# Beginning of a graph-plus-LSTM kernel: the item bias row spread over the partitions by its transfer, nine products of ones ahead of the item quads, and VectorE's first low part ahead of its first item sum

## The chip, the core and the metric

The kernel runs on one core of a Trainium2 chip. The metric is the device time of one execution in microseconds, the median of the runs shown; lower is better.

## The reference

What is computed, cut to what matters here:

```python
# x: 10000 x 128, adj: 10000 x 10000, item_feat: 10000 x 128, all float32
h = item_feat @ W_item.T + b_item              # "items": 10000 x 128, b_item: 128
b = layernorm(x) @ W_user.T + b_user
x = x + relu(adj @ h + b)
x = x + ffn(layernorm(x)[None])[0]             # a one-layer LSTM of 10000 steps, gating, running sums
```

The change concerns the first line only: the bias `b_item`, one row of 128 numbers, is added to every row of the item product.

## The kernel before

**Stages.** The first 1100 us or so compute `adj @ h` for 20 blocks of 500 users (`BW = 500`), with the layer norms and the user product of each block beside it. The items are held as 78 chunks of 128 rows and a tail of 16. For each block, 20 "pieces" of up to 4 chunks of the transposed adjacency stream from memory into `raw` (4 slots). Each piece is worked in two halves of 2 chunks (128 x 1000 numbers): ScalarE rounds a half to its high part `a_hi` (`split_hi`), VectorE subtracts to get the low part `a_lo` (`split_lo`), and TensorE makes three products for each chunk, high x high, low x high and high x low, into `psG` (lines 884 to 886). ScalarE and VectorE write into 4 rotating buffers (`CUT = 4`), so the high part of a later half waits for the products of the half four before it. After the adjacency comes the recurrence.

**The items in block 0.** The items are made during the first block, four chunks (a "quad") at a time: `item_quad(q)` on TensorE writes `psI` (two buffers) from the item features, which land in `u` in ten parts; `item_sum_part(q)` on VectorE adds the bias `bi` and writes `u`; `item_hi_part(q)` on ScalarE rounds to `item_hi`; `item_lo_part(q)` on VectorE subtracts to `item_lo`. The first three adjacency products of a piece need the quad that holds its chunks, high and low (`item_ready`). An item quad is 4 products of 128 x 128 in plain float32, which the profile shows as 8 weight loads and 8 matmuls.

**The beginning.** The order on every engine is written out by hand, and the engines meet by semaphores alone.
- SyncE's queue issues item part 0, then both halves of adjacency piece 0, item part 1, and on.
- ScalarE's queue issues the item weights `wi`, the bias row, the first block of x (`xb`), the user weights `wu` and the user bias. Then ScalarE loads its table and works on half pieces and item high parts as they become ready.
- TensorE makes 8 products of a tile of ones (`keep_at_work(WARM_UP)`, results unused), the bias product, quads 0 and 1, 5 products of ones (`WARM_ON`), the 6 products of the first half piece, quad 2, and on.
- The bias comes as one row into partition 0 (`bi_row`). A product of a row of ones with it (line 944, one row deep) puts the bias into all 128 partitions of the PSUM buffer `psW`, and VectorE copies it to `bi` (line 1336). The row shares its place with `x1_rows`, by which name the trace calls it (`x_rows`).

A product of float32 by float32 appears as two loads and two matmuls, so 8 products of ones are "x16" in the trace.

Of the kernel before, what the change touches and what calls it, by code (L numbers as in the profile page):

```python
# [26 lines left out]
P = 128  # L27
N = 10000
HID = 128
# [43 lines left out]
HI_ONLY = [(q, part) for part in (0, 2) for q in range(4)]  # L73
LO_ONLY = [(q, 1) for q in range(4)]
KEEP_WARM = 8
WARM_UP, WARM_ON = 8, 5
BETWEEN = 4
HANDOVER_TOL = 2.0 ** -19
assert K * L == N and OW % L == 0 and L % 8 == 0 and OW >= 3 * L
# [12 lines left out]
def program(nc, xT, itemT, adj_main, adj_tail, w_itemT, b_item, w_userT, b_user, w_ihT, w_hhT,  # L92
# [13 lines left out]
    with ctx:  # L106
        def sb(name, shape, dt=f32, where=ctx):
            return where.enter_context(nc.sbuf_tensor(name, shape, dt))

        def pb(name, shape, where=ctx):  # L110
            return where.enter_context(nc.psum_tensor(name, shape, f32))

        def sem(name):
            return ctx.enter_context(nc.semaphore(name))
# [5 lines left out]
        ones = sb("ones", [P, P])  # L120
# [5 lines left out]
        bi = sb("bi", [P, HID])  # L126
# [29 lines left out]
        x1_rows = sb("x1_rows", [P, SUB * HID], f32, first)  # L156
        x1b = x1_rows[:, 0:BW]
        wu = x1_rows[:, 0:HID]
        bi_row = x1_rows[0:1, HID:2 * HID]
        normed = x1_rows  # L160
        v_hi = sb("v_hi", [P, BW], f32r, first)
        v_lo = sb("v_lo", [P, BW], f32r, first)
# [16 lines left out]
        psW = pb("psW", [P, 512], first)  # L179
# [44 lines left out]
        wi_in = sem("wi_in")  # L224
        item_tail_ready = sem("item_tail_ready")
        bi_in = sem("bi_in")
        bi_psum = sem("bi_psum")
        bi_ready = sem("bi_ready")
        wu_in = sem("wu_in")
        w_in = sem("w_in")  # L230
        wx_in = sem("wx_in")
# [112 lines left out]
        def cols(c0, n=1):  # L344
            return slice(c0 * BW, (c0 + n) * BW)
# [239 lines left out]
        def _(act):  # L585

            act.dma_start(wi[:, :], w_itemT).then_inc(wi_in, 16)
            act.dma_start(bi_row[:, :], b_item[0:1, :]).then_inc(bi_in, 16)
            act.dma_start(xb[:, 0, :], xT[:, cols(0)]).then_inc(x_in[0], 16)
            act.dma_start(wu[:, :], w_userT).then_inc(wu_in, 16)  # L590
            act.dma_start(bu[:, :], b_user).then_inc(wu_in, 16)
# [262 lines left out]
        def _(pe):  # L854
# [64 lines left out]
            def item_quad(q):  # L919

                if q == 0:
                    pe.wait_ge(wi_in, 16)
                if q in PARTS:
                    pe.wait_ge(item_in[PARTS.index(q)], 16)
                if q >= 2:
                    pe.wait_ge(item_sum, q - 1)
                if q == QUADS - 1:
                    pe.wait_ge(item_tail_ready, 1 + len(STACK))
                for c in range(4 * q, min(4 * q + 4, CH + 1)):
                    rows = P if c < CH else STACKED  # L930
                    columns = u[:, L + c * P:L + (c + 1) * P] if c < CH else item_tail[:, :]
                    last = pe.matmul(psI[0:rows, q % 2, (c % 4) * HID:(c % 4 + 1) * HID], columns, wi[:, :],  # L932
                                     start=True, stop=True)
                last.then_inc(item_psum, 1)
# [5 lines left out]
            pe.wait_ge(ones_ready, 1)  # L940
            keep_at_work(WARM_UP)
            pe.wait_ge(const_ready, 6)
            pe.wait_ge(bi_in, 16)
            pe.matmul(psW[:, 0:HID], ones[0:1, :], bi_row[:, :], start=True, stop=True).then_inc(bi_psum, 1)
            item_quad(0)
            item_quad(1)
            keep_at_work(WARM_ON)
# [176 lines left out]
            with pe.If(redo > 0):  # L1124
                pe.wait_ge(g_restored, 2)
                with nc.tensor.Fori(0, K) as k:
                    with nc.tensor.Fori(0, L) as l:
                        pe.wait_ge(g_h, k * L + l + 1)
                        for q in range(4):
                            for k2, t in enumerate((u_hi, u_lo)):  # L1130
# [3 lines left out]
                                             start=False, stop=True)  # L1134
# [9 lines left out]
        def _(dve):  # L1144
# [32 lines left out]
            def low_user(j):  # L1177
                dve.wait_ge(v_hi_ready, j + 1)
                dve.tensor_tensor(v_lo[:, :], v, v_hi[:, :].bitcast(f32), ALU.subtract).then_inc(v_lo_ready, 1)
# [38 lines left out]
            def item_sum_part(q):  # L1218

                n = min(4, CH + 1 - 4 * q)  # L1220
                dve.wait_ge(item_psum, q + 1)
                if q < QUADS - 1:
                    dst = u[:, L + 4 * q * P:L + (4 * q + n) * P]
                    dve.tensor_tensor(dst.rearrange("p (c h) -> p c h", h=HID),  # L1224
                                      psI[:, q % 2, 0:n * HID].rearrange("p (c h) -> p c h", h=HID),
                                      bi[:, :].unsqueeze(1).to_broadcast([P, n, HID]), ALU.add)\
                        .then_inc(item_sum, 1)
                    return

                dve.memset(sq[:, 0:n * HID], 0.0).then_inc(prep, 1)  # L1230
                dve.wait_ge(prep, 1)
                for c0, c1, a, b in ((0, n - 1, 0, P), *((n - 1, n, a, a + TAIL) for a in STACK)):
                    dve.tensor_tensor(sq[a:b, c0 * HID:c1 * HID].rearrange("p (c h) -> p c h", h=HID),
                                      psI[a:b, q % 2, c0 * HID:c1 * HID].rearrange("p (c h) -> p c h", h=HID),
                                      bi[a:b, :].unsqueeze(1).to_broadcast([b - a, c1 - c0, HID]), ALU.add)\
                        .then_inc(item_sum if a == STACK[-1] else prep, 1)
                dve.wait_ge(prep, 4)

            def item_lo_part(q):
                n = min(4, CH + 1 - 4 * q)  # L1240
                src = u[:, L + 4 * q * P:L + (4 * q + n) * P] if q < QUADS - 1 else sq[:, 0:n * HID]
                dve.wait_ge(item_hi_ready, q + 1)
                last = dve.tensor_tensor(item_lo[:, 4 * q * HID:(4 * q + n) * HID], src,  # L1243
                                         item_hi[:, 4 * q * HID:(4 * q + n) * HID].bitcast(f32), ALU.subtract)
                if q == QUADS - 1:
                    low = slice(STACK[-1], STACKED)
                    own_hi = item_hi[low, CH * HID:(CH + 1) * HID]
                    last.then_inc(prep, 1)
                    dve.wait_ge(prep, 5)
                    last = dve.tensor_tensor(own_hi, sq[low, (n - 1) * HID:n * HID], own_hi.bitcast(f32), ALU.subtract)  # L1250
                last.then_inc(item_ready, 1)
# [31 lines left out]
            def body(j, has2=True, has1=True, items=False):  # L1283
                for r in range(PIECES):
                    if not has1:
                        prepare(r)
                    split_lo(j, r, 0)
                    if items and r == 0:
                        item_lo_part(0)
                        item_sum_part(1)  # L1290
                    if items and 0 < r < QUADS - 2:
                        item_sum_part(r + 2)
                    split_lo(j, r, 1)
                    if items and r == 0:
                        item_sum_part(2)
                    if items and r + 1 < QUADS:
                        item_lo_part(r + 1)
                    if items and r == FIRST["stats"]:
                        stats(0)
                        pair_up(0)  # L1300
                        eps(0)
                    if items and r == FIRST["centred"]:
                        dve.wait_ge(wu_psum, 1)
                        dve.tensor_scalar(wu_hi[:, :], psW[:, 0:HID], 1.0, None, ALU.mult).then_inc(wu_ready, 1)
                        dve.wait_ge(wu_ready, 1)
                        dve.tensor_tensor(wu_lo[:, :], psW[:, 0:HID], wu_hi[:, :].bitcast(f32), ALU.subtract)\
                            .then_inc(wu_ready, 1)
                    if items and r == FIRST["scaled"]:
                        scale_user(0)
                    if r == (FIRST if items else AT)["v_lo"]:  # L1310
                        low_user(j)
                    if has2 and r == AT["scaled"]:
                        scale_user(j)
                    if has2 and r == AT["x1"]:
                        add_relu(j - 1)
                    if has2 and r == AT["stats2"]:
                        stats(2 * j)
                    if has2 and r == AT["pair2"]:
                        pair_up(2 * j)
                    if has2 and r == AT["eps2"]:  # L1320
                        eps(2 * j)
                    if has2 and r == AT["scale2"]:
                        row_scale(2 * j)
                    if has2 and r == AT["apply2"]:
                        apply_rstd(j)
                    if has2 and r == AT["shift2"]:
                        apply_shift(j)
                    if has1 and r == AT["stats1"]:
                        stats(2 * j + 1)
                    if has1 and r == AT["pair1"]:  # L1330
                        pair_up(2 * j + 1)
                    if has1 and r == AT["eps1"]:
                        eps(2 * j + 1)

            dve.wait_ge(bi_psum, 1)
            dve.tensor_copy(bi[:, :], psW[:, 0:HID]).then_inc(bi_ready, 1)
            dve.wait_ge(bi_ready, 1)
            item_sum_part(0)
            body(0, has2=False, items=True)

            body(1)
# [301 lines left out]
```

## Time and profile before

| | |
|---|---|
| median of 3 runs | 1427.13 us (1426.66 to 1427.23) |
| the profiled execution | 1430.41 us |
| its span, first to last instruction | 1428.6 us |
| TensorE busy (PE) | 1405.4 us, 98% of the span |
| weight loads busy (PEld) | 1215.2 us, 85% |
| VectorE busy (DVE) | 1272.8 us, 89% |
| ScalarE busy (ACT) | 1055.8 us, 74% |
| mean granted TensorE clock | 0.993 of full speed |
| read from memory | 432 MB, 310 GB/s over the span |

PE is TensorE's matmuls, PEld its weight loads, which overlap the matmuls; DVE is VectorE, ACT ScalarE, SP SyncE. A "q" behind an engine's name (SPq, ACTq) marks its instruction queue, which issues the transfers. The ends of matmuls are modelled, so the starts of the weight loads are the better clock of what TensorE does. A busy share is a mean over stages: what matters for a change in the first 13 us is which wait ends last there.

### The profile page before, as it was taken

The numbers are of one execution on the slowest core, as the hardware profiler recorded it, in microseconds if no ns is written. First come the engines' busy times: TensorE is split into PE (matmuls) and PEld (weight loads), VectorE is DVE, ScalarE is ACT, GpSimd is POOL, SyncE is SP. The second block draws the span as 40 slices with busy tenths as digits, with TensorE's granted clock in tenths as the row PEclk, the third lists the DMA queues.
The fourth block names the chain that finished last, engine by engine and source line by source line (L and its number), as shares of the span: only waits on it lengthen the run. The fifth ranks groups of instructions, "written<-read, shape, count | busy, mean of one in ns | idle before, by whom it ended". The sixth has DMA issues, their size and how long they took to land.

```text
span 1428.6 us, 26247 instructions
## 1 busy us (share of the span) xinstructions
PE 1405.4 (98%) x7464; PEld 1215.2 (85%) x7464; DVE 1272.8 (89%) x2102; ACT 1055.8 (74%) x1449; POOL 210.0 (15%) x189
## 2 busy tenths in 40 slices
PE   9999999999999999999999999999999999999995
PEld 8878888888888888888888888888888899999994
DVE  7999999999999999999999999999999766676666
ACT  6677787787777777877887877877877676556663
POOL 0000100000000000001001001001000131037775
PEclk9999999999999999999999999999999999999997
DMA  9999999999999999999999999999999203000003
GB/s 375 354 346 379 403 389 387 399 391 374 404 391 382 403 387 381 401 388 398 384 392 392 397 381 402 390 381 401 391 379 386 102 0 144 0 1 1 0 0 144
DMA packets 143466, 442.96 MB, mean 310 GB/s; under 512 B 23944, under 2 KB 43337, under 8 KB 143307
## 3 DMA queue, kind: packets, MB, share of 16 engines
q1 hardware_dynamic: 126048, 426.43, 77.1%
q10 hardware_dynamic: 17387, 16.14, 3.9%
q8 instruction: 17, 0.28, 0.1%
q14 instruction: 14, 0.11, 0.0%
HBM read 432.15 MB, written 10.36 MB: 310 GB/s over the span
## 4 chain that ended last, share of the span: by engine, by line
PE 94%; DVE 5%; ACT 0%; issue 0%; POOL 0%; DVEq 0%; ACTq 0%; POOLq 0%
PE psG L884 24%; PE psG L885 24%; PE psG L886 24%; PE psZ L989 10%; PE psZ L977 3%; PE psZ L975 3%; PE psZ L979 3%; DVE a_lo L1210 2%; PE psZ L995 1%; PE psT L859 1%; PE psI L932 1%; DVE u L1525 1%; DVE item_lo L1243 0%; DVE u L1224 0%; PE psV L938 0%; PE psG L877 0%
## 5 line engine op out<-in xcount | busy, mean ns | idle before, releaser
L667 ACT ACTIVATE a_hi<-raw 128x1000 fp32r<-128x1000 f32 (+1 forms) x800 | 819.1, 1030 | 240.4 <-PE psG L886 222.5
L1210 DVE TENSOR_TENSOR a_lo<-raw,a_hi 128x1000 fp32r<-128x1000 f32 (+1 forms) x800 | 897.0, 1170 | 19.3 <-ACT a_hi L667 14.7
L884 PE MATMUL psG<-a_hi,item_hi 128*128 128x500 f32 x1560 | 610.3, 391 | 1.4 <-DVE a_lo L1210 1.4
L885 PE MATMUL psG<-a_lo,item_hi 128*128 128x500 f32 x1560 | 605.5, 388 | 0.0
L886 PE MATMUL psG<-a_hi,item_lo 128*128 128x500 f32 x1560 | 604.1, 387 | 0.0
L884 PEld LDWEIGHTS psG<-a_hi,item_hi 128*128 128x128 f32 x1560 | 293.2, 188 | 63.3 <-DVE a_lo L1210 2.4
L886 PEld LDWEIGHTS psG<-a_hi,item_lo 128*128 128x128 f32 x1560 | 292.8, 188 | 59.4
L885 PEld LDWEIGHTS psG<-a_lo,item_hi 128*128 128x128 f32 x1560 | 293.3, 188 | 55.5
L989 PE MATMUL psZ<-hist,wh 128*128 (+1 forms) x1264 | 167.9, 276 | 2.9 <-DVE hist L1363 2.2
L989 PEld LDWEIGHTS psZ<-hist,wh 128*128 128x128 f32 x1264 | 154.7, 192 | 3.8 <-issue 2.4
L468 POOL TENSOR_TENSOR row_terms<-var,minus_half 125x4 f32<-125x4 f32 x20 | 37.6, 1879 | 679.8 <-DVE var L1161 679.8
L721 ACT ACTIVATE psZ<-psZ 128x250 f32<-128x250 f32 x158 | 57.3, 363 | 63.6 <-PE psZ L989 61.6
L977 PE MATMUL psZ<-u_lo,wx_hi 128*128 (+1 forms) x312 | 97.9, 315 | 0.0
L975 PE MATMUL psZ<-u_hi,wx_hi 128*128 (+1 forms) x312 | 93.8, 302 | 0.0
L979 PE MATMUL psZ<-u_hi,wx_lo 128*128 (+1 forms) x312 | 87.5, 282 | 0.0
L468 POOL TENSOR_TENSOR rstd<-var,minus_half 125x4 f32<-125x4 f32 x20 | 34.9, 1743 | 331.4 <-DVE var L1161 331.4
L1348 DVE SCALAR_TENSOR_TENSOR psZ<-psZ,C 128x125 f32<-128x125 f32 x158 | 46.6, 295 | 35.8 <-ACT psZ L721 34.7
L1363 DVE SCALAR_TENSOR_TENSOR hist<-go,psZ 128x125 f32 (+1 forms) x160 | 45.5, 284 | 35.0 <-ACT psZ L730 34.4
L725 ACT ACTIVATE go<-psZ 128x250 f32<-128x250 f32 x158 | 59.4, 376 | 6.6 <-PE psZ L989 0.3
L730 ACT ACTIVATE psZ<-C 128x125 f32<-128x125 f32 x158 | 43.6, 276 | 24.2 <-DVE C L1358 20.7
L977 PEld LDWEIGHTS psZ<-u_lo,wx_hi 128*128 128x128 f32 x312 | 59.4, 191 | 0.8
L979 PEld LDWEIGHTS psZ<-u_hi,wx_lo 128*128 128x128 f32 x312 | 59.1, 190 | 0.8
(188 smaller groups left out, 865.4 us busy)
## 6 DMA issues: line engine op xcount, KB each, us to landing
raw<-in_adj_main SPq DMA_DIRECT2D x760, 500.0 KB, 6.7
raw<-in_adj_main SPq DMA_DIRECT2D x40, 250.0 KB, 5.5
sq<-rstd_copy ACTq DMA_DIRECT2D x20, 250.0 KB, 6.7
u<-x_copy SPq DMA_DIRECT2D x1, 5000.0 KB, 14.5
x_copy<-x_rows SPq DMA_DIRECT2D x19, 250.0 KB, 7.2
sq<-rows_copy ACTq DMA_DIRECT2D x19, 250.0 KB, 6.1
un_bb<-rows_copy ACTq DMA_DIRECT2D x19, 250.0 KB, 7.6
u<-in_itemT SPq DMA_DIRECT2D x9, 512.0 KB, 9.4
```

The source lines that it names most:

```text
L468: pool.tensor_tensor(t[:, :], var[:, :], minus_half[0:SW, :].to_broadcast([SW, SUB]), ALU.pow).then_inc(ln_rstd, 1)
L667: nc.scalar.activation(a_hi[:, s % CUT, 0:n], raw[:, r % RAW, at:at + n], ACT.Copy)\
L721: nc.scalar.activation(tb(g, 0, 2).rearrange("p (q k) -> p q k", k=KG), zb(g, 0, par), ACT.Tanh)\
L725: nc.scalar.activation(go[:, g, :].rearrange("p (q k) -> p q k", k=KG), zb(g, 1, par), ACT.Tanh)\
L884: pe.matmul(bank, w_hi, hi, start=(c == 0), stop=False)
L885: pe.matmul(bank, w_hi, lo, start=False, stop=False)
L886: last = pe.matmul(bank, w_lo, hi, start=False, stop=False)
L975: pe.matmul(z, w_hi, hi, start=(q % 2 == 0), stop=False, skip_group_check=True)
L977: pe.matmul(z, w_hi, lo, start=False, stop=False, skip_group_check=True)
L979: pe.matmul(z, w_lo, hi, start=False, stop=False, skip_group_check=True)
L989: last = pe.matmul(psZ[:, 2 * par + bank, at:at + KG], wh[:, q * HID:(q + 1) * HID], hist[:, row, g * KG:(g + 1) * KG], start=False, stop= ...
L1210: last = dve.tensor_tensor(a_lo[:, s % CUT, 0:m], raw[:, r % RAW, at:at + m], a_hi[:, s % CUT, 0:m].bitcast(f32), ALU.subtract)
```

## The change

1. **The bias.** The transfer itself now spreads the row over the 128 partitions: each of 128 rows of `bi` is read from the same 512 bytes in memory. The product on TensorE, the copy on VectorE and two semaphores go. VectorE waits for the transfer (`bi_in`) ahead of its first item sum.
2. **The warm-up.** Nine products of ones ahead of the item quads, instead of eight and the bias product.
3. **VectorE's order.** The first low part of the adjacency, `split_lo(0, 0, 0)`, comes first, and the first item sum behind it.

```diff
--- before.py
+++ after.py
@@ -73,7 +73,7 @@
 HI_ONLY = [(q, part) for part in (0, 2) for q in range(4)]
 LO_ONLY = [(q, 1) for q in range(4)]
 KEEP_WARM = 8
-WARM_UP, WARM_ON = 8, 5
+WARM_UP, WARM_ON = 9, 5
 BETWEEN = 4
 HANDOVER_TOL = 2.0 ** -19
 assert K * L == N and OW % L == 0 and L % 8 == 0 and OW >= 3 * L
@@ -156,7 +156,6 @@
         x1_rows = sb("x1_rows", [P, SUB * HID], f32, first)
         x1b = x1_rows[:, 0:BW]
         wu = x1_rows[:, 0:HID]
-        bi_row = x1_rows[0:1, HID:2 * HID]
         normed = x1_rows
         v_hi = sb("v_hi", [P, BW], f32r, first)
         v_lo = sb("v_lo", [P, BW], f32r, first)
@@ -224,8 +223,6 @@
         wi_in = sem("wi_in")
         item_tail_ready = sem("item_tail_ready")
         bi_in = sem("bi_in")
-        bi_psum = sem("bi_psum")
-        bi_ready = sem("bi_ready")
         wu_in = sem("wu_in")
         w_in = sem("w_in")
         wx_in = sem("wx_in")
@@ -585,7 +582,7 @@
         def _(act):
 
             act.dma_start(wi[:, :], w_itemT).then_inc(wi_in, 16)
-            act.dma_start(bi_row[:, :], b_item[0:1, :]).then_inc(bi_in, 16)
+            act.dma_start(bi[:, :], b_item[0:1, :].to_broadcast([P, HID])).then_inc(bi_in, 16)
             act.dma_start(xb[:, 0, :], xT[:, cols(0)]).then_inc(x_in[0], 16)
             act.dma_start(wu[:, :], w_userT).then_inc(wu_in, 16)
             act.dma_start(bu[:, :], b_user).then_inc(wu_in, 16)
@@ -940,8 +937,6 @@
             pe.wait_ge(ones_ready, 1)
             keep_at_work(WARM_UP)
             pe.wait_ge(const_ready, 6)
-            pe.wait_ge(bi_in, 16)
-            pe.matmul(psW[:, 0:HID], ones[0:1, :], bi_row[:, :], start=True, stop=True).then_inc(bi_psum, 1)
             item_quad(0)
             item_quad(1)
             keep_at_work(WARM_ON)
@@ -1286,6 +1281,8 @@
                         prepare(r)
                     split_lo(j, r, 0)
                     if items and r == 0:
+                        dve.wait_ge(bi_in, 16)
+                        item_sum_part(0)
                         item_lo_part(0)
                         item_sum_part(1)
                     if items and 0 < r < QUADS - 2:
@@ -1332,10 +1329,6 @@
                     if has1 and r == AT["eps1"]:
                         eps(2 * j + 1)
 
-            dve.wait_ge(bi_psum, 1)
-            dve.tensor_copy(bi[:, :], psW[:, 0:HID]).then_inc(bi_ready, 1)
-            dve.wait_ge(bi_ready, 1)
-            item_sum_part(0)
             body(0, has2=False, items=True)
 
             body(1)
```

VectorE's first instructions, before; `a_lo` is the low part of a half piece, `u<-psI,bi` an item sum, `item_lo` an item low part, and brackets hold the semaphores that an instruction waits for:

```order
L1336 COPY bi<-psW 128x128 [waits bi_psum]
L1224 TENSOR_TENSOR u<-psI,bi 128x512 [waits item_psum,bi_ready]
L1210 TENSOR_TENSOR a_lo<-raw,a_hi 128x1000 [waits hi_ready]
L1243 TENSOR_TENSOR item_lo<-u,item_hi 128x512 [waits item_hi_ready]
L1224 TENSOR_TENSOR u<-psI,bi 128x512 [waits item_psum]
L1210 TENSOR_TENSOR a_lo<-raw,a_hi 128x1000 [waits hi_ready]
L1224 TENSOR_TENSOR u<-psI,bi 128x512 [waits item_psum]
L1243 TENSOR_TENSOR item_lo<-u,item_hi 128x512 [waits item_hi_ready]
```

And now (line numbers are 5 lower):

```order
L1205 TENSOR_TENSOR a_lo<-raw,a_hi 128x1000 [waits hi_ready]
L1219 TENSOR_TENSOR u<-psI,bi 128x512 [waits item_psum,bi_in]
L1238 TENSOR_TENSOR item_lo<-u,item_hi 128x512 [waits item_hi_ready]
L1219 TENSOR_TENSOR u<-psI,bi 128x512 [waits item_psum]
L1205 TENSOR_TENSOR a_lo<-raw,a_hi 128x1000 [waits hi_ready]
L1219 TENSOR_TENSOR u<-psI,bi 128x512 [waits item_psum]
L1238 TENSOR_TENSOR item_lo<-u,item_hi 128x512 [waits item_hi_ready]
```

The copy is gone, and the low part of half 0 moved ahead of the first sum; from the first `item_lo` on both orders are the same.

TensorE's first instructions, before (`psV<-ones` are the products of ones, `psW<-x_rows,ones` the bias product, `psI` the item quads, `psG` the adjacency products):

```order
L938 MATMUL psV<-ones 128x128 [waits ones_ready]
L938 MATMUL psV<-ones 128x128 x7
L944 MATMUL psW<-x_rows,ones 128x128 [waits bi_in,const_ready]
L932 MATMUL psI<-wi,u 128x128 [waits item_in0,wi_in]
L932 MATMUL psI<-wi,u 128x128 x7
L938 MATMUL psV<-ones 128x128 x5
L884 MATMUL psG<-a_hi,item_hi 128x500 [waits lo_ready,item_ready]
L885 MATMUL psG<-a_lo,item_hi 128x500
```

And now (line numbers are 3 lower):

```order
L935 MATMUL psV<-ones 128x128 [waits ones_ready]
L935 MATMUL psV<-ones 128x128 x8
L929 MATMUL psI<-wi,u 128x128 [waits item_in0,wi_in,const_ready]
L929 MATMUL psI<-wi,u 128x128 x7
L935 MATMUL psV<-ones 128x128 x5
L881 MATMUL psG<-a_hi,item_hi 128x500 [waits lo_ready,item_ready]
L882 MATMUL psG<-a_lo,item_hi 128x500
```

The bias product with its wait for the bias row is gone, one product of ones is added, and the wait for the constants moved to quad 0.

ScalarE's and SyncE's queues keep their order; in ScalarE's, the second transfer is now `bi<-in_b_item 128x128`.

## Rows read from the trace of the kernel before

**Rows 1.** Windows: busy us by engine (instructions), granted clock, DMA share, GB/s.

```profile
5.43:8.80 3.37, 3.37 (x17) 3.37 (x17) 1.47 (x3) 1.49 (x2) 0.00 (x0) 1.00 1.04 410
...
13.02:80.00 66.98, 66.50 (x361) 56.20 (x359) 66.41 (x99) 46.34 (x55) 3.51 (x6) 1.00 0.97 361
...
86.00:1123.00 1037.00, 1036.55 (x4667) 863.40 (x4666) 986.98 (x1278) 812.36 (x833) 69.98 (x39) 1.00 1.01 388
...
1284.00:1288.00 4.00, 3.29 (x20) 3.09 (x21) 2.44 (x8) 2.93 (x8) 1.88 (x3) 0.81 0.00 0
```

**Rows 2.** The chain that ended last, 5 to 20 us: start, us, what.

```profile
9.21 1.51 PE psV L938 x10
...
13.02 0.69 DVE u L1224
```

**Rows 3.** Timeline, 0 to 45 us: start, us, engine, what, idle before.

```profile
0.75 0.39 SPq L397 DMA_DIRECT2D u<-in_itemT  x1
0.75 0.41 ACTq L587 DMA_DIRECT2D wi<-in_w_itemT  x1
...
1.19 0.91 SPq L409 DMA_DIRECT2D raw<-in_adj_main  x2
...
1.20 0.54 ACTq L588 DMA_DIRECT2D x_rows<-in_b_item  x1
...
1.77 0.38 ACTq L589 DMA_DIRECT2D xb<-in_xT  x1
...
2.18 0.51 ACTq L590 DMA_DIRECT2D x_rows<-in_w_userT  x1
...
5.99 1.04 ACT L667 ACTIVATE a_hi<-raw 128x1000 fp32r<-128x1000 f32 x1 [1.02 <-DMA raw<-in_adj_main]
...
7.62 0.69 DVE L1224 TENSOR_TENSOR u<-psI,bi 128x512 f32<-128x512 f32 x1 [1.79 <-PE psI L932]
8.23 1.19 DVE L1210 TENSOR_TENSOR a_lo<-raw,a_hi 128x1000 fp32r<-128x1000 f32 x1
8.35 0.63 ACT L705 ACTIVATE item_hi<-u 128x512 fp32r<-128x512 f32 x1 [1.32 <-DVE u L1224]
...
9.34 0.68 DVE L1243 TENSOR_TENSOR item_lo<-u,item_hi 128x512 fp32r<-128x512 f32 x1
...
13.02 0.69 DVE L1224 TENSOR_TENSOR u<-psI,bi 128x512 f32<-128x512 f32 x1 [1.30 <-PE psI L932]
```

**Rows 4.** Timeline of TensorE's weight loads, 0 to 12 us.

```profile
1.00 3.48 PEld L938 LDWEIGHTS psV<-ones 128*128 128x128 f32 x16 [1.00 <-POOL ones L455]
4.71 0.50 PEld L944 LDWEIGHTS psW<-x_rows,ones 1*128 1x128 f32 x2 [0.22 <-issue]
5.43 3.49 PEld L932 LDWEIGHTS psI<-wi,u 128*128 128x128 f32 x16 [0.23 <-issue]
8.80 1.74 PEld L938 LDWEIGHTS psV<-ones 128*128 128x128 f32 x10
10.46 0.19 PEld L884 LDWEIGHTS psG<-a_hi,item_hi 128*128 128x128 f32 x1
...
11.71 0.41 PEld L932 LDWEIGHTS psI<-wi,u 128*128 128x128 f32 x2
```

**Rows 5.** Transfers by line: KB each, us from issue to landing.

```profile
u<-in_itemT SPq DMA_DIRECT2D x1, 512.0 KB, 4.0
wi<-in_w_itemT ACTq DMA_DIRECT2D x1, 64.0 KB, 4.1
...
raw<-in_adj_main SPq DMA_DIRECT2D x1, 500.0 KB, 4.8
...
xb<-in_xT ACTq DMA_DIRECT2D x1, 250.0 KB, 6.3
...
x_rows<-in_w_userT ACTq DMA_DIRECT2D x1, 64.0 KB, 7.4
```

**Rows 6.** Timeline of TensorE's weight loads, 10.3 to 10.5 us.

```profile
10.12 0.41 PEld L938 LDWEIGHTS psV<-ones 128*128 128x128 f32 x3
```

## Prediction

> **What bounds the kernel now.** I began with windows of the span. From 86 us to 1123 us TensorE is busy 1036.55 of 1037 us [rows 1]. The reader is to see that nothing in the beginning can change what that stretch costs; it can only make it start earlier or later. From 13.02 to 80 us VectorE is busy 66.41 of 66.98 us and TensorE 66.50 [rows 1]: both are close to full, so a shift of the whole pattern passes through to the end, and a shift of one engine alone would not.
>
> So the question is what sets the start of VectorE's unbroken work. The chain that ended last runs through TensorE's queue, the late warm-up products among it, into VectorE's third item sum at 13.02 [rows 2]. VectorE had waited 1.30 us for that sum [rows 3], and everything of it follows from there.
>
> Under that chain lie the weight loads of TensorE [rows 4] and the timeline of VectorE and ScalarE [rows 3]. The first big product's load began at 10.46. Its two conditions were met before: the low part of item quad 0 ended at 9.34 + 0.68 = 10.02, the low part of the first half piece at 8.23 + 1.19 = 9.42. So TensorE's own queue came last: quad 0 began only at 5.43, and the five products behind quad 1 ended at about 10.46. That is the queue from which the change takes the bias product.
>
> **The change, part by part.**
>
> *The bias product on TensorE.* Its two loads began at 4.71, and the first load of quad 0 at 5.43; ahead of each stands a short idle time, 0.22 and 0.23 us, that no recorded event explains [rows 4]. Now a ninth product of ones fills a part of that place. One load every 3.37 / 16 = 0.211 us (5.43 to 8.80 for 16) lets 18 loads end at 1.00 + 3.80 = 4.80. The first item transfer landed at 0.75 + 4.0 = 4.75, the item weights at 0.75 + 4.1 = 4.85 [rows 3, 5]. So quad 0 can begin at 4.89 at the earliest, and at 5.43, as before, if the stall comes with the waits and not with the bias product. I take 5.0, by the landings, which are the nearer rows. Both quads then end at 5.0 + 3.37 = 8.37.
>
> *The clock.* The granted clock stands at 1.00 for 5.43 to 8.80 too [rows 1], yet loads came every 0.21 us there and every (0.41 - 0.19) / 2 = 0.11 us from 10.12 on [rows 6]: the levels of 1.2 and of 2.4 GHz. Ten loads from 8.80 to 10.46 are about six at 0.21 and four at 0.11, which puts the rise near 9.9. Until then TensorE had worked without a pause since 5.43, and had paused twice before that. With the rise at 9.9 again, the ten loads now are seven at 0.21 and three at 0.11: they end at 8.37 + 1.80 = 10.17. With an earlier rise they end earlier still; with quad 0 at 5.43 they end at 10.46 as before.
>
> *VectorE's order.* The copy of the bias goes; it lay inside VectorE's wait for quad 0, 1.79 us that ended at 7.62 [rows 3], and is worth nothing. The low part of the first half piece now stands ahead of the first item sum. It can start when ScalarE's high part is done, 5.99 + 1.04 = 7.03, plus a hand-over of 0.04 (the first sum ended at 7.62 + 0.69 = 8.31, ScalarE's item high part began at 8.35): 7.07. The next instruction starts 1.11 later (8.23 to 9.34): the first sum at 8.18, which is 0.56 **later** than the 7.62 of before, although quad 0 is done sooner. From there: sum done 8.87; item high part on ScalarE 8.91 to 9.54; item low part on VectorE 9.58 to 10.26, against 10.02 before. Before, that low part was held back by the adjacency's until 9.34, 9.34 - 8.98 = 0.36 after its own input was ready; now it waits for its input. With 0.05 for the hand-over the first big product begins at 10.31.
>
> *The sum.* TensorE's queue is free at 10.17, VectorE's item low part allows 10.31: the last wait has changed hands, and the gain is 10.46 - 10.31 = 0.15 us, or 0 if quad 0 still begins at 5.43. The path behind keeps its length: six big products 11.71 - 10.46 = 1.25 [rows 4], then quad 2, and the third sum 13.02 - 10.46 = 2.56 after the first big product, at 12.87. VectorE is there in time: after the item low part at 9.58 come the second sum at 10.18 and the second low part at 10.78, and it is free at 11.89. So 0.98 us of its old 1.30 of idle time is left, and that cover also hides a second sum that would come 0.9 late.
>
> *The bias by its transfer.* It stays second in ScalarE's queue, but moves 64 KB in 128 rows and not 0.5 KB in one. The transfers around it bound its landing: as fast as the item weights (64 KB, 4.1 us) it lands at 1.20 + 4.1 = 5.30; as slow as the user weights (64 KB, 7.4 us) at 8.60, 0.42 after the sum wants it [rows 3, 5]. I take about 5.5 to 6: it stands right behind the item weights, and ahead of x, which landed at 1.77 + 6.3 = 8.07. So it is hidden by the low part, which keeps VectorE until 8.18. Issuing 128 rows took ScalarE 0.41, the one row 0.54: no loss there.
>
> What it may push is the first half piece of the adjacency, which landed at 1.19 + 4.8 = 5.99 [rows 3, 5] and from which the new path now hangs. Lower bound 0: x was waiting in ScalarE's queue in any case, so the bias takes x's place in time, not the half piece's. Between: 64 KB at 410 GB/s [rows 1] is 0.16 us. Upper bound: the user weights, also 64 KB, landed at 2.18 + 7.4 = 9.58, 1.5 us behind x; were the half piece held back as long, everything would move by 1.5. I take 0, for the first reason.
>
> The Trainium skill, "DMA: Bandwidth & Descriptors", section "Bandwidth", calls transfers under 64 KB dominated by their descriptors and measures 0.95 us for 64 KB; by it, were all of that ahead of the half piece, the result would be 0.95 - 0.15 = 0.8 us slower. The same page's section "Queues, rings and completion order" has a DMA engine alternate between the queues that have work, which is how I read it above; no row here tells the two apart.
>
> Against what time: the profiled execution took 1430.41 us, 1.8 of it outside its span of 1428.6, and stands 3.3 above the median of 1427.13. Some of that may be in its late part, where the granted clock was 0.81 between 1284 and 1288 us [rows 1]; the beginning has none in it. I take 0.15 off the median: 1427.0 us.
>
> **The rivals.**
>
> *A, the forecast: VectorE's chain takes over, a small gain.* Between 1427.13 (none) and 1426.9. Chance 0.66.
>
> *B: the clock is the prize.* The timed runs need not have had the rise at 9.9. Where it comes only after quad 2, the old path pays 4 loads of 0.10, 1.25 for six big products at half the rate and 8 loads of 0.10: 2.45 us. With the pauses filled the rise may come before that: 1427.13 - 0.15 - 2.45 = 1424.5 at best, about 1425.8 if half the runs had it. For it: the pauses ahead of quad 0 are the only ones before the rise. Against it: the three runs lie within 0.57 us, which a clock that moves the path by 2.45 would spread; and with the rise of the profiled run, an earlier one gives nothing beyond A, since the first sum waits for the low part until 8.18 however soon quad 0 is done. Chance 0.12. The Trainium skill, "TensorE: Matmul & The Clock Gate", section "What's actually happening", has the throttled state as the default and activity as what releases it; the trace agrees in so far as the loads grow shorter after an unbroken stretch.
>
> *C: slower, through the first half piece.* The bias transfer holds back its landing by more than 0.15 us, or itself lands after 8.33. Time: from 1427.15 up to 1427.0 + 1.5 = 1428.5. For it: before, the low part could have begun at 7.07 and began at 8.23, so the half piece had 1.16 to spare, and now it has nothing. Against it: x's place in the queue. Chance 0.16.
>
> *D: the time moves by more than the beginning can make it,* in either direction, by the late clock or by how the changed code lies. Chance 0.06.
>
> **How the numbers follow.** 0.2% of 1427 is 2.85 us, about what a measurement of this kernel can tell from no change. A, B and C lie inside it. Faster by over 0.2%: 0.01 of B, where the slow stretch is longer than I priced, and 0.03 of D: 0.04. Slower: 0.03 of D. Within: 0.93. The range of 1425.4 to 1428.3 takes A, most of C and two thirds of B. With the spread of the three runs, A's own range is 1426.6 to 1427.4.
>
> **What would show it.** In the new trace: no copy on VectorE; quad 0's first load near 5.0; the adjacency low part at 7.07, the first sum at 8.2, the item low part ending near 10.26; the first big product near 10.31, released by the item low part and not by TensorE's own queue; the third sum at about 12.87. Loads every 0.11 us before 9 us would be B's clock. ScalarE's first high part after 6.1, or a first sum that waits for a transfer, would be C and make me wrong, as would a third sum before 12.6.

## The result: 0.25% slower

| | before | changed |
|---|---|---|
| median of 12 runs | 1427.39 us (1426.44 to 1431.05) | 1431.2 us (1430.0 to 1433.1) |
| profiled execution, its span | 1430.41, 1428.6 | 1430.81, 1429.0 |

The ratio is 1.0025, with a 95% interval from 1.0017 to 1.0033: 3.6 us slower, between 2.4 and 4.7. I had forecast 1427.0 and a range up to 1428.3.

The two spans differ by 0.4 us only, so the spans alone would have hidden the loss. Read from the front, the traces agree with the medians. In the timeline of TensorE's weight loads of either kernel, at the first products of the recurrence, the changed kernel is 1131.72 - 1128.08 = 3.64 us behind:

```profile
1128.08 0.52 PEld L989 LDWEIGHTS psZ<-hist,wh 128*128 128x128 f32 x4 [0.84 <-DVE hist L1363]
```

```profile
1131.72 0.41 PEld L984 LDWEIGHTS psZ<-hist,wh 128*128 128x128 f32 x3 [0.84 <-DVE hist L1356]
```

Two things behind the changed part then favoured the changed kernel's profiled run. The clock that was down around 1286 us in the kernel before [rows 1] stayed up in it, and late in the recurrence the same weight load is only 1408.14 - 1406.07 = 2.07 us behind. And between VectorE's last instruction (at 1422.91 and 1424.97) and the end of the span lie 5.7 and 4.0 us. Each is worth about 1.6 us, and neither goes with the beginning: of the 13 traces here, five have the long end and eight the short one, and two (the kernel before and e12) have the low clock near 1286 us. The same may happen in the runs that were only timed, which spread over as much as 5.1 us for one kernel (e12); no trace shows those. This is why the experiments below are read first by places in the trace.

The profile after. VectorE's timeline (start, us, engine, what, idle before), which answers to [rows 3]:

```profile
9.01 1.20 DVE L1205 TENSOR_TENSOR a_lo<-raw,a_hi 128x1000 fp32r<-128x1000 f32 x1 [9.01 <-ACT a_hi L664]
10.13 0.68 DVE L1219 TENSOR_TENSOR u<-psI,bi 128x512 f32<-128x512 f32 x1
11.51 0.69 DVE L1238 TENSOR_TENSOR item_lo<-u,item_hi 128x512 fp32r<-128x512 f32 x1 [0.69 <-ACT item_hi L702]
...
16.27 0.69 DVE L1219 TENSOR_TENSOR u<-psI,bi 128x512 f32<-128x512 f32 x1 [2.36 <-PE psI L929]
```

The third sum stands at 16.27 and not at 13.02. ScalarE's first high part, in its timeline, waited 2.98 us for its half piece and began at 7.94, not 5.99:

```profile
7.94 1.04 ACT L664 ACTIVATE a_hi<-raw 128x1000 fp32r<-128x1000 f32 x1 [2.98 <-DMA raw<-in_adj_main]
```

TensorE's weight loads, against [rows 4]:

```profile
1.00 3.91 PEld L935 LDWEIGHTS psV<-ones 128*128 128x128 f32 x18 [1.00 <-POOL ones L452]
5.03 2.39 PEld L929 LDWEIGHTS psI<-wi,u 128*128 128x128 f32 x16
7.33 1.20 PEld L935 LDWEIGHTS psV<-ones 128*128 128x128 f32 x10
12.25 0.19 PEld L881 LDWEIGHTS psG<-a_hi,item_hi 128*128 128x128 f32 x1 [3.72 <-DVE item_lo L1238]
...
13.49 0.33 PEld L883 LDWEIGHTS psG<-a_hi,item_lo 128*128 128x128 f32 x1
```

Quad 0 did begin at 5.03, and the clock rose sooner: the 16 loads of the quads took 2.39 us in place of 3.49. But then TensorE was idle for 3.72 us, and a load at 13.49 takes 0.33 us again. Windows of the changed kernel (as [rows 1], the last three numbers being granted clock, DMA share and GB/s) show both troubles:

```profile
4.00:5.00 1.00, 1.00 (x6) 0.91 (x5) 0.00 (x0) 0.95 (x2) 0.00 (x0) 1.00 0.96 336
5.00:6.00 1.00, 1.00 (x5) 0.97 (x5) 0.00 (x0) 0.00 (x0) 0.00 (x0) 1.00 0.63 147
6.00:7.00 1.00, 1.00 (x11) 1.00 (x10) 0.00 (x0) 0.00 (x0) 0.00 (x0) 1.00 0.66 164
7.00:8.00 1.00, 1.00 (x11) 1.00 (x10) 0.00 (x0) 0.06 (x1) 0.00 (x0) 1.00 0.92 351
...
13.00:16.40 3.40, 3.40 (x13) 3.04 (x13) 1.04 (x2) 2.32 (x3) 0.00 (x0) 0.50 1.03 415
```

In the kernel before, 5 to 7 us moved 412 GB/s; here it is 147 and 164, and TensorE ran at half its clock from 13.0 to 16.4. The issues say which transfer it was: the 64 KB of the bias took 7.1 us from issue to landing, longer than the half megabyte of adjacency beside it.

```profile
raw<-in_adj_main SPq DMA_DIRECT2D x1, 500.0 KB, 6.7
bi<-in_b_item ACTq DMA_DIRECT2D x1, 64.0 KB, 7.1
```

The chain that ended last of the changed kernel opens accordingly:

```profile
1.19 6.73 DMA raw<-in_adj_main
7.94 1.05 ACT a_hi L664
...
10.13 0.69 DVE u L1219
10.85 0.64 ACT item_hi L702
11.51 0.70 DVE item_lo L1238
```

### The profile page after: what moved, and what is told of

The parts are those of the page before. It is cut to its first block, busy times and chain, and to the rows that moved or that the text cites. A ratio compares the mean times of both kernels' runs of the same rounds, so it can differ in the third digit from the quotient of the medians.

```text
span 1429.0 us, 26245 instructions
## 1 busy us (share of the span) xinstructions
PE 1403.9 (98%) x7464; PEld 1213.3 (85%) x7464; DVE 1272.9 (89%) x2101; ACT 1056.2 (74%) x1449; POOL 212.8 (15%) x189
## 4 chain that ended last, share of the span: by engine, by line
PE 90%; DVE 6%; DMA 2%; issue 1%; ACT 1%; POOL 0%; SPq 0%; DVEq 0%; ACTq 0%
PE psG L881 23%; PE psG L882 23%; PE psG L883 22%; PE psZ L984 10%; DVE a_lo L1205 3%; PE psZ L970 3%; PE psZ L972 3%; PE psZ L974 3%; DMA raw<-in_adj_main 2%; PE psZ L990 1%; PE psT L856 1%; DVE item_lo L1238 1%; DVE u L1518 1%; PE psI L929 1%; DVE u L1219 0%
```

## The theory, its rivals and the experiments

**Theory T** (S, with which I began, is its first part alone): (1) 128 reads of the same 512 bytes hold up the transfer engines for both queues, and the first half piece with them; (2) VectorE's new order leaves nothing to hide that and makes the first big product late by itself; (3) in the idle time this leaves behind quad 1, TensorE's clock falls. **Q**: 64 KB more in 128 small rows would do the same. **R**: the reorder alone costs it all.

All ratios are against the kernel before on the same chip: 11 runs of each kernel against 27 or 33 of the kernel before, whose median was 1427.62 us for e1, e2, e4 and e5, 1427.47 for e3, e7, e8 and e10, and 1427.52 for e6, e12 and the second run of e7. The ratios are not quotients of these medians; for e12 the two differ most (1.0006, and 1.0015 by the medians). "First big product" is its load on TensorE: 10.46 before, 12.25 changed. "Third sum" is VectorE's: 13.02 and 16.27. From the third sum to the first weight load of the recurrence shown above it is 1114.9 to 1115.9 us in twelve of the 13 traces (1117.4 in e12), so the place of the third sum tells how late the recurrence starts to within about half a microsecond.

**1. The bias from 128 rows of its own (run e1).** The input holds 128 equal rows; the rest is the changed kernel.

```diff
-            act.dma_start(bi[:, :], b_item[0:1, :].to_broadcast([P, HID])).then_inc(bi_in, 16)
+            act.dma_start(bi[:, :], b_item).then_inc(bi_in, 16)
```

> The changed kernel, but each of the 128 partitions reads its own copy of the bias row: the input is laid out as 128 equal rows, still 64 KB in 128 rows of 512 bytes, in the same place of ScalarE's queue. Theory S (the slow thing is 128 reads of the same 512 bytes, which hold up the transfer engines for both queues): bytes moved between 5 and 7 us go back from 155 GB/s to about 400, the first half piece lands near 6.1 and not at 7.9, the first big product begins at 10.3 to 10.5, TensorE idles under 2 us ahead of it, no fall of the clock at 13 us, and the time is 1427.0 to 1427.5. Theory Q (64 KB more in ScalarE's queue, or 128 small rows, are enough): the first half piece still lands at 7.5 to 7.9, first big product at 12, time 1430 to 1431.

Measured: 1428.74 us, ratio 1.0008 (0.9999 to 1.0017), above the 1427.0 to 1427.5 that I expected. Windows of this run:

```profile
5.00:6.00 1.00, 0.96 (x8) 0.99 (x9) 0.00 (x0) 0.06 (x1) 0.00 (x0) 1.00 1.04 391
6.00:7.00 1.00, 1.00 (x11) 1.00 (x10) 0.00 (x0) 0.78 (x1) 0.00 (x0) 1.00 0.99 402
...
10.80:14.20 3.40, 3.40 (x12) 2.86 (x12) 1.39 (x2) 2.48 (x3) 0.00 (x0) 0.50 1.03 412
```

Its first big product on TensorE, and its third sum on VectorE:

```profile
10.54 0.19 PEld L881 LDWEIGHTS psG<-a_hi,item_hi 128*128 128x128 f32 x1 [2.55 <-DVE item_lo L1238]
14.68 0.69 DVE L1219 TENSOR_TENSOR u<-psI,bi 128x512 f32<-128x512 f32 x1 [2.48 <-PE psI L929]
```

No dip in the rate: the high part began at 6.22, the first big product at 10.54, and the bias landed after 5.4 us in place of 7.1. Same bytes, same row size, same place in the queue: Q falls, part 1 stands. (Whether the reads must be of the very same bytes, or only of few places close together, no run tells.) But I had also expected under 2 us of idle time and no fall of the clock, and it fell, from 10.8 to 14.2, after 2.55 us in which TensorE waited; the third sum came at 14.68. That miss gave part 3 of the theory.

**2. The order alone (run e2).** The kernel before, with `split_lo(j, 0, 0)` ahead of the copy of the bias and the first item sum.

```diff
                     split_lo(j, r, 0)
                     if items and r == 0:
+                        dve.wait_ge(bi_psum, 1)
+                        dve.tensor_copy(bi[:, :], psW[:, 0:HID]).then_inc(bi_ready, 1)
+                        dve.wait_ge(bi_ready, 1)
+                        item_sum_part(0)
                         item_lo_part(0)
...
-            dve.wait_ge(bi_psum, 1)
-            dve.tensor_copy(bi[:, :], psW[:, 0:HID]).then_inc(bi_ready, 1)
-            dve.wait_ge(bi_ready, 1)
-            item_sum_part(0)
```

> The kernel before with the third edit alone: the bias still comes by its one row, the product and the copy, but VectorE's first low part stands ahead of the copy and the first item sum; eight products of ones. Theory S and Q alike (the transfer is the cause): the first half piece lands at 6.0 as before, low part at 7.07, copy and first sum at about 8.2 and 8.5, item low part done near 10.5, first big product at 10.5 to 10.7 against 10.46, time 1427.1 to 1427.6. Rival R (the reorder costs the time): first big product after 11.5 and 1430.

Measured: 1428.9 us, ratio 1.0008 (0.9999 to 1.0017); first big product at 10.54, third sum at 13.11. R falls as the whole cause: the median is 1.3 us above the kernel before's, and the changed kernel's 3.8. In this execution the clock rose late, as in the profiled kernel before, TensorE was idle for 0.15 us only ahead of the first big product, and the order cost 0.09 us. The median stands higher than I expected, by 1.3 us, though its interval still reaches no change. Where the clock rises early the old order gains and this one does not, and behind the longer idle time the clock falls (e1, and 7 below); no trace shows this very kernel with an early clock, so that this is what lifts its median is argued and not shown.

**3. One dose of the same-row read in the kernel before (run e4).** A transfer that nothing needs, into a place that is loaded later (ScalarE waits for it ahead of that load).

```diff
+            act.dma_start(wh[:, 0:HID], b_item[0:1, :].to_broadcast([P, HID])).then_inc(extra_in, 16)
```

> The kernel before plus one transfer that nothing needs, right behind the bias row in ScalarE's queue: the bias row spread over 128 partitions, 64 KB, all from the same 512 bytes. Theory S: the rate falls to about 150 GB/s between 5 and 7 us, the first half piece lands at 7.6 to 8.0. The old order of VectorE hides a part of it (the low part began at 8.23): low part at about 9.0, first big product at 10.6 to 11.3, third sum 0.2 to 1 us late, time 1427.4 to 1428.4. Theory Q: the same. It tells S from the reorder: if the half piece still lands at 6.0, the spread is not the cause.

**4. The same dose from 128 different rows (run e5).**

```diff
+            act.dma_start(wh[:, 0:HID], w_userT).then_inc(extra_in, 16)
```

> The kernel before plus one unneeded transfer in the same place, of the same 64 KB in 128 rows of 512 bytes, but from 128 different rows (the user weights). Theory S: no dip in the rate, the first half piece lands at 6.0 to 6.2, everything as before, 1427.1 to 1427.6. Theory Q: as with the same row, the half piece lands at 7.6 to 8.0.

Measured: e4 1427.98 us, ratio 1.0004 (0.9995 to 1.0013); e5 1427.56, ratio 0.9998 (0.9989 to 1.0007). Windows, e4 first:

```profile
6.00:7.00 1.00, 1.00 (x11) 1.00 (x10) 0.48 (x1) 0.93 (x1) 0.00 (x0) 1.00 0.71 175
7.00:8.00 1.00, 1.00 (x11) 1.00 (x10) 1.00 (x2) 0.75 (x2) 0.00 (x0) 1.00 0.70 186
```

```profile
6.00:7.00 1.00, 1.00 (x12) 1.00 (x11) 0.73 (x2) 0.93 (x2) 0.00 (x0) 1.00 1.07 419
7.00:8.00 1.00, 1.00 (x11) 0.97 (x9) 1.00 (x1) 1.00 (x2) 0.00 (x0) 1.00 1.01 406
```

The dip belongs to the shared row. I had its place wrong: this transfer was issued 0.57 us later than the bias of the changed kernel, the dip came 1 us later, and the first half piece had landed before it (high part at 6.07). First big product: 9.00, not the 10.6 to 11.3 that I expected; that the time of e4 came out inside its range is luck. What was in flight behind it was held up instead: ScalarE's second high part began at 9.20 against 7.53 in e5, and the third sum stood at 12.39 against 11.36. The third sum itself was late by the next part of the item features, for which quad 2 waited in e4 and did not in e5 (10.05):

```profile
11.19 0.97 PEld L935 LDWEIGHTS psI<-wi,u 128*128 128x128 f32 x8 [0.98 <-DMA u<-in_itemT]
```

So the price depends on what is in flight when the reads begin. Both third sums are ahead of the 13.02 of the kernel before, since in both executions the clock rose early: the 16 loads of the quads took 1.86 us, against 3.49 [rows 4].

**5. Two doses (run e12).** The line of e4 twice.

> The kernel before plus two unneeded transfers behind the bias row, each of them the bias row spread over 128 partitions from the same 512 bytes. With one of them the rate fell to 175 and 186 GB/s from 6 to 8 us and was back by 9. Theory S: with two the low rate lasts about twice as long, 3.5 to 4.5 us, about 128 slow reads each; second half piece of piece 0 at 11 to 12 and not at 9.2, third sum at 13 to 15, time 1428.5 to 1430. If the dip is a start-up cost and not a cost of each read, it lasts 2 us again and the time is that of one dose, about 1428.

Measured: 1429.62 us, ratio 1.0006 (0.9997 to 1.0015). Windows:

```profile
6.00:7.00 1.00, 1.00 (x12) 1.00 (x11) 0.29 (x1) 0.99 (x2) 0.00 (x0) 1.00 0.80 226
7.00:8.00 1.00, 1.00 (x12) 1.00 (x11) 1.00 (x2) 0.56 (x1) 0.00 (x0) 1.00 0.89 233
8.00:9.00 1.00, 0.61 (x6) 0.41 (x4) 1.00 (x2) 0.36 (x2) 0.00 (x0) 1.00 0.73 199
9.00:10.00 1.00, 0.83 (x4) 0.72 (x5) 0.94 (x3) 1.00 (x2) 0.00 (x0) 1.00 0.90 281
```

The low rate lasts four microseconds and not two, though it is less low: measured against 410 GB/s, the windows leave about 0.70 MB unmoved from 6 to 10 us, and those of e4 about 0.46 MB from 6 to 8: by this estimate 1.5 times and not twice. That speaks for a cost of each read. It does not rule out a start-up cost that every transfer from a shared row pays for itself; e5 shows only that a transfer from 128 rows pays none. The second half piece came at 8.71, earlier than I expected, and the third at 13.72, where ScalarE waited 3.34 us for it. The third sum, at 13.02, was held up by quad 2, which waited 1.47 us for its item features and began at 11.82. The loads of the recurrence begin at 1127.17 in e5, 1128.00 with one dose and 1130.39 with two.

**6. TensorE kept at work (runs e10 and e6).** Products of ones behind quad 1 fill the idle time. The first edit is that of run e10, to the kernel of e1; the second is that of run e6, to the changed kernel.

```diff
-WARM_UP, WARM_ON = 9, 5
+WARM_UP, WARM_ON = 9, 16
...
-WARM_UP, WARM_ON = 9, 5
+WARM_UP, WARM_ON = 9, 21
```

> The kernel of run e1 (bias from 128 rows of its own, new order of VectorE) with 16 instead of 5 products of ones behind quad 1, so that TensorE works on until the first big product. In e1 TensorE was idle for 2.5 us, its clock fell from 10.8 to 14.2 us, and the third sum began at 14.7. Theory T: no fall of the clock, first big product at 10.5 to 10.7, third sum at 13.0 to 13.2, so 1.5 us ahead of e1, time 1427.0 to 1427.8. If the clock falls all the same, third sum at 14.7 and 1428.5 to 1429.

> The changed kernel with 21 instead of 5 products of ones behind quad 1, so that TensorE works on until the first big product. In the changed kernel it was idle for 3.7 us, its clock fell from 13.0 to 16.4 us, and the third sum began at 16.27. Theory T: the half piece lands at 7.9 again, first big product at 12.2 to 12.4, no fall of the clock, third sum at 14.8 to 14.9, 1.4 us ahead of the changed kernel; time 1429 to 1430. If the fall of the clock has another cause than the idle time, third sum at 16.3 and 1431.

Measured: e10 1428.82 us, ratio 1.0009 (1.0000 to 1.0018); e6 1429.04, ratio 1.0012 (1.0003 to 1.0021), against 1.0025 of the changed kernel. Windows, e10 and then e6:

```profile
10.50:14.00 3.50, 3.50 (x20) 3.07 (x20) 2.60 (x4) 2.85 (x5) 0.00 (x0) 1.00 1.01 390
```

```profile
12.60:16.00 3.40, 3.40 (x22) 3.02 (x21) 2.04 (x4) 2.63 (x4) 0.00 (x0) 1.00 1.04 417
```

Their third sums, e10 and then e6:

```profile
13.07 0.69 DVE L1219 TENSOR_TENSOR u<-psI,bi 128x512 f32<-128x512 f32 x1 [0.90 <-PE psI L929]
```

```profile
15.14 0.69 DVE L1219 TENSOR_TENSOR u<-psI,bi 128x512 f32<-128x512 f32 x1 [1.36 <-PE psI L929]
```

No fall of the clock in either. The third sum is 14.68 - 13.07 = 1.61 us earlier than in e1 and 16.27 - 15.14 = 1.13 earlier than in the changed kernel. In e6 the added products ran a little too long: the first big product began at 12.59, 0.34 us behind that of the changed kernel, though its item low part was ready 0.13 us sooner. From the first big product to the third sum it is 2.56 and 2.55 us (2.56 before), and was 4.02 in the changed kernel: 1.46 us is the price of the fall (in e1, 4.14 and so 1.58). The idle time is its cause: nothing but its filling was changed, in two pairs of kernels, and of the 13 traces the clock fell here in the three with 2.55 us or more of idle time and in no other. For e10 the median did not follow the trace, and its range of 1427.0 to 1427.8 was missed; 11 runs that spread over 3.7 us don't settle a difference of 1.6.

**7. The old order with the two transfers (runs e3 and e7).** The changed kernel, and the kernel of e1, each with VectorE's first item sum in its old place.

```diff
-                        dve.wait_ge(bi_in, 16)
-                        item_sum_part(0)
...
+            dve.wait_ge(bi_in, 16)
+            item_sum_part(0)
             body(0, has2=False, items=True)
```

> The changed kernel with its third edit undone: the spread from one row and nine products stay, but VectorE waits for the spread and makes the first item sum ahead of its first low part. Theory T (two costs: the same-row spread holds up the transfers by 1.7 us, and the new order leaves TensorE idle, behind which its clock falls): the spread lands at about 8.2, so the first sum begins at 8.3 and not at 5.1 + quad time, low part at 8.9 if the half piece landed by 7.9, item low part at about 10.0, first big product at 10.7; TensorE is idle for about 2.2 us ahead of it, less than the 3.7 of the changed kernel. Third sum 13.3 without a fall of the clock, 14.7 with one. Time 1427.5 to 1429, faster than the changed kernel by 2 to 3. Theory S alone (the spread is all of the loss): first big product at 12.2 again and 1430 to 1431.

> The changed kernel with the bias from 128 equal rows of its own and with VectorE's old order. Theory T: neither cost is left. Quad 0 begins near 5.0; with a clock that rises before 6 us the first sum is at 6.3 to 7.0, the first big product at 8.8 to 9.2, TensorE idles under 1.2 us ahead of it, no fall of the clock, third sum at 11.4 to 11.8 (13.02 in the profiled kernel before). Time 1425.5 to 1427.2, ratio to before 0.9985 to 1.0000. Theory S: as e1, where the new order stood, 1427.5 to 1428.7.

Measured: e3 1429.19 us, ratio 1.0011 (1.0002 to 1.002); e7 1426.51 us, ratio 0.9995 (0.9986 to 1.0004). VectorE's timeline, e3 and then e7:

```profile
8.22 0.69 DVE L1219 TENSOR_TENSOR u<-psI,bi 128x512 f32<-128x512 f32 x1 [8.22 <-DMA bi<-in_b_item]
8.83 1.19 DVE L1205 TENSOR_TENSOR a_lo<-raw,a_hi 128x1000 fp32r<-128x1000 f32 x1
...
14.81 0.69 DVE L1219 TENSOR_TENSOR u<-psI,bi 128x512 f32<-128x512 f32 x1 [2.48 <-PE psI L929]
```

```profile
6.72 0.69 DVE L1219 TENSOR_TENSOR u<-psI,bi 128x512 f32<-128x512 f32 x1 [6.72 <-PE psI L929]
7.33 1.20 DVE L1205 TENSOR_TENSOR a_lo<-raw,a_hi 128x1000 fp32r<-128x1000 f32 x1
...
11.74 0.69 DVE L1219 TENSOR_TENSOR u<-psI,bi 128x512 f32<-128x512 f32 x1 [0.91 <-PE psI L929]
```

In e3 the first sum waits for the bias itself, the first big product is at 10.67, TensorE was idle 2.77 us and its clock fell to 0.50 from 10.8 to 14.1: third sum 14.81. In e7 all three costs are gone, and the third sum is at 11.74. So the order alone, with the clock up in both, is e10 against e7: 13.07 - 11.74 = 1.33 us.

Four traces with an early rise of the clock now cross the two costs. The third sum, and behind it the first load of the recurrence:

| | bias from one row | bias from 128 rows |
|---|---|---|
| VectorE's new order | changed: 16.27, 1131.72 | e1: 14.68, 1129.66 |
| VectorE's old order | e3: 14.81, 1129.74 | e7: 11.74, 1126.89 |

Either one alone costs about 3 us (3.07 the shared row, 2.94 the order), and both together 4.53 and not 6: each alone leaves TensorE idle long enough for the clock to fall, and with both it falls once.

**8. The product kept, behind quad 0 (run e8).**

```diff
-WARM_UP, WARM_ON = 8, 5
+WARM_UP, WARM_ON = 9, 5
...
+            item_quad(0)
             pe.wait_ge(bi_in, 16)
             pe.matmul(psW[:, 0:HID], ones[0:1, :], bi_row[:, :], start=True, stop=True).then_inc(bi_psum, 1)
-            item_quad(0)
```

> The kernel before with nine products of ones and its bias product moved behind quad 0: the 0.5 KB row, the product, the copy and VectorE's old order stay. No 64 KB transfer at all. Theory T: quad 0 begins near 5.05 and not at 5.43, half piece landed by 6.0; with a clock that rises before 6.5 us the first sum at 6.8 to 7.3, first big product near 9.0, third sum near 11.6; time 1425.5 to 1427.3. If the stall ahead of quad 0 came with the waits and not with the product, quad 0 begins at 5.4 again and the time is that of before.

Measured: 1426.98 us, ratio 0.9994 (0.9985 to 1.0003). Quad 0 began at 4.94, the first big product came at 9.76 and not near 9.0, and the third sum at 12.31, not at 11.6: copy and sum came behind the product, at 6.98 and 7.31.

**9. Run e7 again.**

> The kernel of run e7 again (bias from 128 equal rows of its own, nine products of ones, VectorE's old order), to see whether it beats the kernel before. First big product at 8.7 to 9.3, third sum at 11.3 to 11.8, 1.2 to 1.7 us ahead of the profiled kernel before; since the kernel before has such a start in some of its executions, the median should stand 0.5 to 1.2 us below it, 1426.3 to 1426.9.

Measured: 1427.91 us, ratio 0.9999 (0.999 to 1.0008), first big product at 9.09, third sum at 11.65. The trace does what it should, the median not: it lies 1.4 us above that of the same kernel in 7. Neither this kernel nor e8 can be told from the kernel before by time, so none is claimed to beat it.

## Why the prediction was wrong

- **The step that failed** is the bound on the bias transfer: "I take 0, for the first reason", and with it the landing at "about 5.5 to 6". The bias landed at 1.20 + 7.1 = 8.3 and the first half piece at 7.9, 1.95 us late. The landing of the bias itself cost nothing, since VectorE came to its first sum at 10.13 only; the term that failed is the 0 for the half piece. I had taken the item weights for its nearest row: 64 KB, 128 rows of 512 bytes. The row I lacked was one that reads the same bytes 128 times. My upper bound of 1.5, from the user weights, was the right kind of number and still too small. The Trainium skill's 0.95 us for 64 KB ("DMA: Bandwidth & Descriptors", section "Bandwidth", measured there for transfers that GpSimd issues) was too small a price too. That an engine alternates between the queues (the same page, section "Queues, rings and completion order") did not protect the other queue here: the first half piece came through SyncE's queue, the bias through ScalarE's. The shared row cost the changed kernel 12.25 - 10.54 = 1.71 us at the first big product (e1 against it).
- **Rival C had the mechanism** ("held back by more than 0.15 us", "now it has nothing to spare") at chance 0.16, but ended at 1428.5, since it knew no second cost behind it; a kernel slower by over 0.2% had 0.03, by D alone, and not by the way it came.
- **The second cost was not in the prediction at all.** I had worked out that an earlier clock "gives nothing beyond A", and stopped there. It leaves TensorE idle behind quad 1, longer the sooner it is done, and behind that idle time the clock fell: 1.46 us. Rival B looked at what a rise could give and not at what would fall again. The Trainium skill, "TensorE: Matmul & The Clock Gate", section "HAM oscillation — how this bites in real kernels", warns of kernels whose clock falls again in their waits; the trace agrees, with 0.50 from 13.0 to 16.4.
- **VectorE's order** was read rightly: "the last wait has changed hands". First sum one low part (1.12) after its start, item low part behind ScalarE: in e1 and e2 the first big product came at 10.54, 0.2 later than the 10.31 I gave, most of it the half piece's landing and in e2 the copy. What I missed is the other side: I compared with an execution whose clock rose at 9.9. Where it rises early, the old order starts the first big product at 8.81 (e5), and the new one can't before 10.5.
- **TensorE's queue**: quad 0 at 5.0: right (5.03, and 4.92 to 5.20 in the seven other traces without the product ahead of it). That the stall belonged to the product is not shown: with the product in its place quad 0 began at 4.99 in e5 and 5.25 in e4, and an idle time of 0.29 to 0.53 us without a recorded event stands ahead of quad 0 in e1, e3, e6, e10 and the second run of e7, which have no product. The reading by the landings is the one that holds.
- **The clock's rise** differs between executions: the 16 loads of quads 0 and 1 took 3.49 us in the profiled kernel before and in e2, and 1.86 to 2.78 in the changed kernel, e1, e3 to e7, e10 and e12, in either order and with either transfer. So the length of the old path is not one number. My "three runs within 0.57 us" was too few to see that: 12 runs spread over 4.6.
- **The sum from the places in the trace**: 1.71 for the same-row read, 0.08 for the rest up to the first big product and 1.46 for the fall of the clock are the 3.25 between the third sums at 13.02 and 16.27, on a path that the order had laid bare. Up to the recurrence it has become 3.64; where the other 0.39 came from was not looked into. The split holds only against an execution with a late clock, where the order itself costs 0.1. Against an early clock the order costs 1.3, or 2.9 with the fall of the clock behind it, and the changed kernel reaches the recurrence 1131.72 - 1127.17 = 4.55 later than e5, the kernel before with a transfer that does no harm. The measured 3.6 us has an interval, 2.4 to 4.7, that holds both 3.64 and 4.55; how often the kernel before has which clock was not measured, so the mean share of each cost stays open.

## What to carry to other kernels

A spread of one memory row over all partitions was not like another load of 64 KB: it slowed whatever was in flight beside it. Two ways avoided that here: a row in memory for each partition (e7), or the row brought once and spread on the chip (the kernel before, e8). When a change makes an engine ready sooner, ask what it then waits for and whether that idle time costs its clock; in the traces a fill of unneeded products was worth 1.6 and 1.1 us. And before an order is changed so that work A hides the arrival of B, check the other pairing: the first item sum was the head of the longer chain, and with an early clock its input was there first (6.72 in e7, while the low part could begin at about 7.3).

## What the runs showed of the hardware

- 128 reads of 512 bytes from one address, amid other transfers, brought the rate of all of them from about 410 down to between 147 and 203 GB/s for 2 us (changed kernel, e3, e4, e6), two such spreads to between 199 and 281 GB/s for 4 us (e12). From 128 addresses: 391 to 419 GB/s (e1, e5).
- TensorE's clock fell to half after idle times of 2.55, 2.77 and 3.7 us at the same place of the program, and not after 0.75 to 1.16 us (e4, e5, e7 both times, e8, e12), nor after another 1.47 us a little later in e12.
- From VectorE's last instruction to the end of the span lie either 3.9 to 4.3 or 5.6 to 5.7 us, by execution. The cause was not looked into.
